# A decoder layer on one core: stages behind attention placed by lags and measured durations, queries turned two heads at a time

## The reference

```
x = x + layernorm(attention(layernorm(x))) * g2  # 16 query heads of 64, one shared key/value head, causal; q, k of unit length
x = x + cross_attention(layernorm(x), ctx)       # 16 heads of 16, no mask
x = x + experts(layernorm(x))                    # 4 experts, gate*sigmoid(gate)*value, hidden 1024; each token goes to the argmax expert
```

## Time and profile before

| | before |
|---|---|
| median of 3 runs | 1004.83 us (1004.71 to 1005.0) |
| profiled execution | 1004.88 us, of which the span of its instructions 1003.1 us |
| TensorE busy | 886.8 us, 88% |
| VectorE busy | 588.5 us, 59% |
| ScalarE busy | 580.2 us, 58% |
| GpSimd busy | 194.3 us, 19% |
| mean granted TensorE clock | 0.956 |

### The profile page before, as it was taken

One profiled execution on the slowest core, in us unless ns is written; L12 is line 12 of the kernel. 1 busy time (PEld: TensorE's weight loads), 2 busy tenths in 40 slices (PEclk: granted clock), 3 DMA queues, 4 the chain that ended last, 5 costly groups with the idle time before them and its releaser, 6 DMA issues.

```text
span 1003.1 us, 14623 instructions
## 1 busy us (share of the span) xinstructions
PE 886.8 (88%) x4510; PEld 676.9 (67%) x4510; DVE 588.5 (59%) x1369; ACT 580.2 (58%) x1144; POOL 194.3 (19%) x220
## 2 busy tenths in 40 slices
PE   4699999999999998889999999999771199999997
PEld 2566677677777775766777777776550178888885
DVE  4556778667677667667676676848586132323231
ACT  1586858778788776558686777778443022222221
POOL 3223221112111113113121111101103401111111
PEclk9799999999999999999999999999975599999999
DMA  8400000002000000000000000220123201010100
GB/s 274 79 2 1 1 1 1 1 1 85 1 1 2 1 1 0 1 1 1 1 1 1 1 1 1 88 81 1 64 93 122 84 1 33 19 32 21 32 16 10
DMA packets 19177, 29.04 MB, mean 29 GB/s; under 512 B 2079, under 2 KB 15648, under 8 KB 19104
## 3 DMA queue, kind: packets, MB, share of 16 engines
q1 hardware_dynamic: 17008, 22.73, 7.5%
q0 software_dynamic: 1680, 4.21, 1.2%
q10 hardware_dynamic: 416, 1.18, 0.3%
HBM read 21.41 MB, written 7.10 MB: 28 GB/s over the span
## 4 chain that ended last, share of the span: by engine, by line
PE 42%; DVE 4%; issue 3%; POOL 2%; ACT 1%; DMA 0%; DVEq 0%; ACTq 0%; POOLq 0%
PE W L1323 7%; PE S L1300 6%; PE O L1300 5%; PE O L1140 2%; PE S L1122 2%; PE S L1121 2%; PE O L1137 2%; PE O L1138 2%; PE W L1211 2%; PE W L1253 2%; POOL sorted_rows L602 2%; PE W L1233 1%; PE W L1179 1%; PE W L1311 1%; PE S L1311 1%
## 5 line engine op out<-in xcount | busy, mean ns | idle before, releaser
L860 DVE TENSOR_TENSOR pl<-pr,ph 128x512 fp32r<-128x512 f32 x288 | 199.5, 697 | 75.2 <-ACT pr L652 59.6
L651 ACT ACTIVATE ph<-S 128x512 fp32r<-128x512 f32 x288 | 174.1, 605 | 107.3 <-PE S L1122 104.0
L652 ACT ACTIVATE pr<-S 128x512 f32<-128x512 f32 x288 | 173.2, 601 | 0.0
L1137 PE MATMUL O<-ph,vhi 128*65 128x512 f32 x288 | 137.2, 476 | 0.0
L1140 PE MATMUL O<-pl,vhi 128*65 128x512 f32 x288 | 114.6, 398 | 10.0 <-DVE pl L860 9.7
L1122 PE MATMUL S<-qT,kT 128*128 128x512 f32 x288 | 114.0, 396 | 0.0
L1121 PE MATMUL S<-qT,kT 128*128 128x512 f32 x288 | 113.2, 393 | 0.0
L1138 PE MATMUL O<-ph,vlo 128*65 128x512 f32 x288 | 113.2, 393 | 0.0
L566 POOL TENSOR_TENSOR rn<-ssc,half 128x17 f32<-128x17 f32 x16 | 54.2, 3388 | 150.4 <-DVE ssc L891 145.1
L555 POOL TENSOR_TENSOR rs<-ri,half 128x1 f32<-128x1 f32 x48 | 36.7, 764 | 234.9 <-DVE ri L798 234.9
L768 ACT ACTIVATE gate<-S 128x512 f32<-128x512 f32 x38 | 20.6, 595 | 102.7 <-PE S L1300 102.7
(11 more groups left out here) (174 smaller groups left out, 1642.8 us busy)
## 6 DMA issues: line engine op xcount, KB each, us to landing
raw<-in_w_v SPq DMA_DIRECT2D x16, 512.0 KB, 4.0
wps<-in_w_proj SPq DMA_DIRECT2D x4, 1024.0 KB, 9.5
sorted_rows<-pad_row SPq DMA_DIRECT2D x19, 128.5 KB, 4.1
xs<-sorted_rows SPq DMA_DIRECT2D x19, 128.5 KB, 2.1
wqkv<-in_wqkv_t ACTq DMA_DIRECT2D x1, 1152.0 KB, 6.5
wout<-in_wout_t SPq DMA_DIRECT2D x1, 1024.0 KB, 10.0
xall<-in_x SPq DMA_DIRECT2D x1, 1024.0 KB, 11.0
xall<-in_x SPq DMA_DIRECT2D x1, 768.0 KB, 8.1
```

Of the source, the lines that this page charges most:

```text
L651: nc.scalar.activation(ph[:, k % RING, :], S[k % AHEAD][:], ACT.Exp, scale=SIM_SCALE).then_inc(ph_ready, 1)
L652: nc.scalar.activation(pr[:, k % RING, :], S[k % AHEAD][:], ACT.Exp, scale=SIM_SCALE)\
L860: nc.vector.tensor_tensor(pl[:, k % RING, :], pr[:, k % RING, :], ph[:, k % RING, :].bitcast(F32), ALU.subtract).then_inc(pl_ready, 1)
L1137: nc.tensor.matmul(o, vhi[:, vs, 0:DH + 1], ph[:, k % RING, :], start=j == 0, stop=False)
```

## The change

- **Order.** `STAGES` keeps only the stages ahead of and inside attention. The stages behind a tile's attention stand in `CHAIN`: each with the stage it follows and a lag in positions, counted from the tile's last attention step. `HAZARDS` lists for each the readers in an earlier tile that it must stay behind. `COST` holds a duration for each stage on VectorE, ScalarE and TensorE; a stage moves on to the next position while the two before, two after and its own hold more VectorE or ScalarE work than time. After the last slot come 90 positions without a step in place of three slots of eight. With lags summed, a tile's chain is 60 positions long.
- **Queries.** `q_high` and `qhl` go. `q_turn` turns the normed queries two heads at a time, in two stages of four transposes and one for the doubled key. ScalarE copies the high parts out of PSUM, even heads into rows 0 to 63 and odd heads into rows 64 to 127 of `qT`; `q_low`, now behind `q_turn` and on VectorE, subtracts them from the bank and writes each low part to the other half's rows. The bank is free after `q_low`. `lows_early` moves a `q_low` ahead of the stage that would need its bank. The value's low part is a subtraction on GpSimd.
- **Roots.** Each of the three kinds has its own ring of two.
- **Weights.** Eleven units in place of ten are split early, each behind a named stage of the last tile.
- Some small buffers move to other addresses.

```diff
-    ("heads_out", 3, -1, 1), ("probs_turn", 0, -3, 1), ("q_norm", 0, 1, 2), ("probs_turn", 1, -3, 2),
-    ("z2_turn", 0, -2, 3), ("q_norm", 1, 1, 3), ("out_turn", 0, -1, 5.5), ("probs_turn", 2, -3, 4), ("q_high", 0, 1, 4),
...
+    ("q_norm", 0, 1, 2), ("q_norm", 1, 1, 3), ("k_double", 0, 1, 4), ("v_parts", 0, 1, 5), ("q_turn", 0, 1, 7), ("q_low", 0, 1, 8),
+    ("norm_x", 0, 2, 7), ("heads_out", 0, 0, 9), ("z_turn", 0, 2, 11), ("q_turn", 1, 1, 11), ("q_low", 1, 1, 12),
+    ("q_turn", 2, 1, 14), ("q_low", 2, 1, 15), ("heads_out", 1, 0, 17), ("qkv", 0, 2, 19), ("qkv", 1, 2, 21),
+    ("qkv_squares", 0, 2, 22), ("qkv", 2, 2, 23), ("qkv_squares", 1, 2, 24), ("heads_out", 2, 0, 25),
+    ("qkv_sums", 0, 2, 26), ("qkv_sums", 1, 2, 28),
...
+CHAIN = [
+    ("heads_out", 3, None, 2), ("out_turn", 0, ("heads_out", 3), 4), ("out_turn", 1, ("out_turn", 0), 1),
+    ("out_proj", 0, ("out_turn", 1), 4), ("xa_norm", 0, ("out_proj", 0), 3), ("x1_stats", 0, ("xa_norm", 0), 3),
+    ("z2_norm", 0, ("x1_stats", 0), 3), ("z2_turn", 0, ("z2_norm", 0), 3), ("xq", 0, ("z2_turn", 0), 4),
+    ("scores", 0, ("xq", 0), 4), ("scores", 1, ("scores", 0), 1), ("probs_exp", 0, ("scores", 1), 1),
+    ("scores", 2, ("scores", 1), 2), ("scores", 3, ("scores", 2), 1), ("probs_exp", 1, ("scores", 3), 1),
+    ("probs_sum", 0, ("probs_exp", 0), 2), ("probs_sum", 1, ("probs_exp", 1), 2), ("probs_turn", 0, ("probs_exp", 1), 4),
+    ("probs_turn", 1, ("probs_turn", 0), 1), ("probs_turn", 2, ("probs_turn", 1), 1), ("probs_v", 0, ("probs_turn", 2), 4),
+    ("xo_turn", 0, ("probs_v", 0), 3), ("xattn_out", 0, ("xo_turn", 0), 4), ("x2_norm", 0, ("xattn_out", 0), 3),
+] + [("logits", e, ("logits", e - 1) if e else ("x2_norm", 0), 1) for e in range(EXP)]
+HAZARDS = {
...
+COST = {
...
+STEP = (0.7, 1.2, 1.16)
+IDLE = 1.5
+NEAR = 2
+TAIL = 90
...
+EARLY = {0: None, 1: ("out_turn", 0), 2: ("out_turn", 1), 3: ("xa_norm", 0), 4: ("z2_norm", 0), 5: ("z2_turn", 0), 6: ("xq", 0),
+         7: ("probs_sum", 1), 8: ("probs_turn", 0), 9: ("probs_turn", 2), 10: ("probs_v", 0)}
+EARLY_UNITS = len(EARLY)
...
+def lows_early(here):
+    owed = []
+    for stages in here:
+        n = 0
+        while n < len(stages):
+            name, part, t = stages[n]
+            if name in READER:
+                for entry in owed:
+                    entry[1] += 1
+                for key, _ in [entry for entry in owed if entry[1] >= WB]:
+                    for later in here:
+                        if key in later:
+                            later.remove(key)
+                    n = stages.index((name, part, t))
+                    stages.insert(n, key)
+                    n += 1
+                owed = [entry for entry in owed if entry[1] < WB]
+                if name == "q_turn":
+                    owed.append([("q_low", part, t), 0])
+            elif name == "q_low":
+                owed = [entry for entry in owed if entry[0] != (name, part, t)]
+            n += 1
...
+    load = [[sum(COST[entry[2]][e] for entry in entries) for e in range(3)] for entries in placed]
+    at_of = {}
+    def full(at, e, cost):
+        near = range(at - NEAR, min(at + NEAR + 1, last))
+        steps_near = sum(positions[n] is not None for n in near)
+        time = sum(load[n][2] + (IDLE if positions[n] is None else 0) for n in near) + (STEP[2] - STEP[e]) * steps_near
+        return load[at][e] > 0 and sum(load[n][e] for n in near) + cost > time
+    for t in range(TILES):
+        end = positions.index(start[GROUPS * (t + 1)] - 1)
+        for order, (name, part, behind, lag) in enumerate(CHAIN):
+            at = end + lag if behind is None else at_of[(*behind, t)] + lag
+            if t > 0:
+                at = max(at, at_of[name, part, t - 1])
+            for other, its_part, back in HAZARDS.get((name, part), []):
+                if t >= back:
+                    at = max(at, at_of[other, its_part, t - back])
+            while at < last and name not in ("heads_out", "out_turn") and any(COST[name][e] and full(at, e, COST[name][e]) for e in range(2)):
+                at += 1
+            at_of[name, part, t] = at
+            put(at, name, part, t, order)
+            for e in range(3):
+                load[at][e] += COST[name][e]
...
+                        nc.gpsimd.tensor_copy(vhi[:, vs, 0:DH], qn[:, HEADS + 1, :]).then_inc(v_ready, 1)
+                        pool.wait_ge(v_ready, 2 * t + 1)
+                        nc.gpsimd.tensor_tensor(vlo[:, vs, 0:DH], qn[:, HEADS + 1, :], vhi[:, vs, 0:DH].bitcast(F32),
+                                                ALU.subtract).then_inc(v_ready, 1)
...
-                        nc.scalar.copy(qhl[:, part * QH:(part + 1) * QH, 0, :], qn[:, part * QH:(part + 1) * QH, :])\
-                            .then_inc(qhi_ready, 1)
-                    elif name == "q_turn" and part < 4:
+                    elif name == "q_turn" and part < 2:
                         act.wait_ge(side_ready, job + 1)
                         if t >= 2:
                             act.wait_ge(s_ready, group_start[GROUPS * (t - 1)])
-                        nc.scalar.copy(qT[t % 2][:, 4 * part:4 * part + 4, :].rearrange("p h q -> p (h q)"),
-                                       W[job % WB][:]).then_inc(act_freed, 1)
-                    elif name == "q_turn" and part == 4:
+                        for rows, heads in halves_of(part):
+                            nc.scalar.copy(qT[t % 2][rows, heads, :], W[job % WB][rows, :].rearrange("p (h q) -> p h q", q=P))\
+                                .then_inc(qth_ready, 1)
+                    elif name == "q_turn" and part == 2:
                         act.wait_ge(side_ready, job + 1)
                         if t >= KV:
                             act.wait_ge(s_ready, group_start[GROUPS * TPB * ((t - KV) // TPB + 1)])
-                        nc.scalar.copy(kT[:, t % KV].rearrange("p a k -> p (a k)"), W[job % WB][:, 0:2 * P])\
-                            .then_inc(act_freed, 1)
+                        nc.scalar.copy(kT[:, t % KV, 0, :], W[job % WB][:, 0:P]).then_inc(qth_ready, 1)
...
+                    elif name == "k_double":
+                        dve.wait_ge(qn_ready, 2 * t + 2)
+                        if t >= 2:
+                            dve.wait_ge(side_ready, job_count("q_turn", 2, t - 2))
+                        nc.vector.tensor_copy(kdup[:, t % 2], qn[:, HEADS, :].unsqueeze(1).broadcast_to([P, 2, DH])).then_inc(kdup_ready, 1)
                     elif name == "q_low":
-                        heads = slice(part * QH, (part + 1) * QH)
-                        dve.wait_ge(qhi_ready, 2 * t + part + 1)
-                        nc.vector.tensor_tensor(qhl[:, heads, 1, :], qn[:, heads, :], qhl[:, heads, 0, :].bitcast(F32),
-                                                ALU.subtract).then_inc(qlo_ready, 1)
-                        if part == 1:
-                            dve.wait_ge(qlo_ready, 2 * t + 2)
-                            nc.vector.tensor_copy(kdup[:], qhl[:, HEADS].bitcast(F32).unsqueeze(2).broadcast_to([P, 2, 2, DH]))\
-                                .then_inc(kdup_ready, 1)
+                        bank = W[job_of["q_turn", part, t] % WB]
+                        if part < 2:
+                            for n, (rows, heads) in enumerate(halves_of(part)):
+                                other = slice(DH, P) if n == 0 else slice(0, DH)
+                                dve.wait_ge(qth_ready, 5 * t + 2 * part + n + 1)
+                                low = nc.vector.tensor_tensor(qT[t % 2][other, heads, :],
+                                                              bank[rows, :].rearrange("p (h q) -> p h q", q=P),
+                                                              qT[t % 2][rows, heads, :].bitcast(F32), ALU.subtract)
+                                low.then_inc(dve_freed if n else qtl_ready, 1)
+                        else:
+                            dve.wait_ge(qth_ready, 5 * t + 5)
+                            nc.vector.tensor_tensor(kT[:, t % KV, 1, :], bank[:, 0:P], kT[:, t % KV, 0, :].bitcast(F32),
+                                                    ALU.subtract).then_inc(dve_freed, 1)
...
-                        pe.wait_ge(qlo_ready, 2 * t + 2)
-                        pe.wait_ge(kdup_ready, t + 1)
+                        pe.wait_ge(qn_ready, 2 * t + (2 if part else 1))
+                        if part == 2:
+                            pe.wait_ge(kdup_ready, t + 1)
                         freed_wait(pe, job)
-                        for h in range(4 if part < 4 else 2):
-                            src = qhl[:, 4 * part + h].bitcast(F32) if part < 4 else kdup[:, h]
-                            mm = nc.tensor.transpose(W[job % WB][:, h * P:(h + 1) * P], src.rearrange("p a d -> p (a d)"),
-                                                     ident[:])
+                        for c in range(4 if part < 2 else 1):
```

(19 more changed lines are left out.)

200 lines of the change are left out of this document (94 added, 106 removed).

## The result

The changed kernel takes 997.63 us (median of four runs, 996.16 to 1001.04). The kernel before took 1004.77 beside it (1004.16 to 1005.0). The ratio is 0.9928, with a 95% interval from 0.9911 to 0.9945: faster by 7 us. The forecast was 20 us, so the direction was right and the size was off by 13. The profiled execution of after is the longest of its four (1001.04, with a span of 999.3; its mean granted clock was 0.939, that of the others 0.941, 0.944 and 0.944). The traces alone therefore differ by only 4 us, and sums from them stand some 3 us above the median.

The account below looks back on a forecast made before the run. TensorE was taken to bound the kernel, busy 88% of the span. 16.9 + 7 - 3 - 6.6 + 5.6 = 19.9 us saved, so 1004.9 - 19.9 = 985.0 us, range 969 to 999.

Parts of the forecast that it names:

- A bank is held longer: Turns' PSUM banks, held 1.9 to 2.7 us instead of 0.59: TensorE waits in six small tiles, 3 us lost.
- the granted clock 1.00 between 80 and 690: Sign of being right: TensorE keeps its full clock from 80 to 690 us, nearly all of attention.
- Rival C: Small tiles: bank waits cost 14.4 us instead of 3, no idle won beyond 5; 998.4 us, chance 0.14.
- B: Rival: small tiles fill up, no bank is waited for, tail set by dependencies alone; 965.6 us, chance 0.18.
- D: Rival: every turn, in large tiles too, makes TensorE wait for its bank; slower, 1010.8 us, chance 0.07.
- The transposes: TensorE turns 9 instead of 18 per tile and drops two of five turning stages: 16.9 us saved.
- The order: Chains spread over about 60 positions fill TensorE's idle time in small tiles: 7 us gained.
- Work that moves ahead: Work of tiles 13 and 14 moves from the tail into saturated attention: 6.6 us more TensorE time there.
- the tail: From last value matmul to last logit: tile 15's chain ends at 47 instead of 52.6 us, 5.6 less.
- VectorE's 24 us more: VectorE's extra subtractions, 1.5 us per tile, 24 in all: covered by its free time, counted at nothing.

Follow-up runs that it names:

- e1: Changed kernel with the low parts subtracted in SBUF, coming out zero, so ScalarE's copies free the bank: 981.88 us, 0.9756 of the kernel before.
- e3: Kernel before, its order of stages kept, with the new turn of the queries two heads at a time: 1005.04 us, 0.9994 of the kernel before.
- e9: Kernel before's order with the new turn and the bank freed by ScalarE's copies, low parts zero: 995.08 us, 0.9909 of the kernel before.
- e4: Changed kernel's new order with the old turn, queries split before they are turned: 1001.01 us, 0.9974 of the kernel before.
- e7: Changed kernel with the planner's shifts of stages off for tiles 12 to 15: 1005.96 us, 1.0000 of the kernel before.
- e10: e8 plus 24 needless matmuls in front of the last tile's stages in the tail: 990.46 us, 0.9856 of the kernel before.
- e8: Changed kernel with a turn's subtraction ahead of the very next job instead of the third: 990.41 us, 0.9846 of the kernel before.
- e2: Changed kernel with a turn's subtraction ahead of the second next job instead of the third: 991.32 us, 0.9852 of the kernel before.

## Why the prediction missed, by its own steps

**The step that failed** is "A bank is held longer: I take 3 us in all, because there TensorE has idle time already". The named waits are 11.2 us, and behind two of them TensorE ran slower, which the step priced at nothing and which "the granted clock 1.00 between 80 and 690" denied. Measured by e1, the held bank costs 15.7 us by the medians and 17 by the ratios. For the small tiles the 3 us were about right: 2.4. The reasoning failed for the large ones, at "three jobs take about 4 positions of 1.2 us or more: covered": 8.8 us of the waits are there, the longest of 3.03 in tile 7, which has 32 positions. That compared mean rates. The release stands in VectorE's queue behind other stages that themselves wait for TensorE (the timeline at 327 to 333). The bounds (0 to 38) held the cost, but they were worked out for the small tiles alone. Rival C, "the banks eat half", is what came, at 998.4 against 997.6, at a chance of 0.14. Its picture was right as to the bank, but it too placed the waits in the small tiles, and the clock's share wasn't in it: that its number fits is luck in part. Of the others, B needed no wait for a bank: e1 is that case, and its idle is 23.8, not the 13.6 that B wanted. D wanted every turn to wait, in large tiles too; 12 waits stand against its 48. Attention ended at 703.0, forecast 693.

Had I taken 15.7 in place of 3, the sum would have been 985.0 + 12.7 = 997.7, and 999 with 17; that the sum then fits so closely is luck, as the other terms show.

**The transposes** (16.9) held: 19.0 by after's trace, 19.5 by e1's, and in the old order 14.3 by e3's and 12.9 by e9's, all with the estimate for the clock in them. **The order** (7 of idle) held in kind: with the bank free, idle is 9.8 us under before's (23.8 against 33.6). In after the waits for the bank took as much again, and the idle time shows no change at all. With the old turn (e4) the order takes only 2.5 us of idle.

**Work that moves ahead** (6.6) was too large, and so was **the tail** (5.6). The step said that a chain is over in 60 positions. I read the lags and left out the shifts that the planner adds when an engine's surroundings are full. With them the chain of tile 13 takes 75 positions and that of tile 14 takes 64. Tile 13's product with the values still lies in the tail's first moments. The tail of after, as in the earlier trace rows, its last value matmul having ended at 703.0:

```profile
702.82 2.31 PE L1348 MATMUL W<-vb,pT 128*128 128x128 f32 x20
...
712.61 3.69 PE L1306 MATMUL W<-wout,onT 128*128 128x256 f32 x16 [1.76 <-DVE sc L1042]
...
726.87 1.92 PE L1320 MATMUL W<-z2T,wq 128*128 128x128 f32 x8
...
742.39 4.47 PE L1348 MATMUL W<-vb,pT 128*128 128x128 f32 x20 [1.10 <-ACT pT L823]
```

Only 20 records, some 2.2 us, went ahead. From the end of the last value matmul the projection starts at 9.6 (forecast 8.0, before 6.9), the query projection at 23.9 (19.7, before 22.8), the product at 39.4 (34.4, before 38.4). The scaling behind it no longer waits for other tiles' logits, as foreseen (43.9, forecast 37 to 39, before 44.4), but the product now runs at the low level, 4.47 for 2.42. The two errors nearly cancel: 6.6 - 5.6 was to cost 1.0 net, and 2.2 - 0.5 cost 1.7. In e4 tile 13's chain takes 64 positions, its product lies ahead of the last step, and the tail is 48.9, near the 47 of the forecast.

**VectorE's 24 us more** are not what made the change fall short: e1 has them too and is 17 us faster. In after the two subtractions of 689 ns take 1.41 from first start to last end, and the next instruction starts at 332.91: nothing overlaps, and some 0.03 us pass between two. The two of 753 in the earlier trace rows overlap by 0.085. Lost overlap is thus 0.115 us each. It isn't the wait that stands between the two subtractions: two `pl` of 128 rows with waits between them overlap too (in e1 1.29 us for two of 0.70, at 326.72). The Trainium skill, "VectorE: DVE Perf Modes", section "Two Vector instructions with no wait between them", has just this hold for an instruction on other partitions; my estimate from it was 0.08. The trace agrees in kind; e1 bears the same holds.

**What stays open.** e1 still spends 23.9 us of attention at the low level against 10.2 before, beside waits for `z`, `pl`, `sc` and `qn`. It isn't the new order's alone: e4 has 17.1 and e9 13.7. The two stretches near 120 and 160 us stand in every version with both the new order and the new turn, and in none with only one of them; no run took this apart. How much of the tail is owed to the clock is open as well (e4, e7, e10).

**The best whole version** is e8, the subtraction in front of the next job (e2 is within its spread): 0.9846 of before, against 0.9928 for the change as made. e1 shows that up to another 0.9% lies in a release that costs no engine anything. Going through SBUF doesn't reach it.

## What to carry to other kernels

When the reader of a shared buffer changes, price how long the buffer is then held, and follow the release through its engine's queue: what stands ahead of it, and whether that waits for the engine that wants the buffer. Do this in the dense stretches too, where mean rates say that there is time. Put such a release directly behind its producer, ahead of anything that waits. A short wait of TensorE in a saturated stretch can cost a second time, for the work behind it at the lower clock, but not each one does: compare several executions before putting a price on it. And read a planner's placement from its result, not from its table of lags.

## What the hardware showed that I had not expected

TensorE at 95% busy over attention (633 of 667 us) still fell to 1.2 GHz behind single waits of 1.6 to 3.0 us. Behind the wait of 2.49 for `qn`:

```profile
398.71 0.85 PE L1284 MATMUL W<-ident,qn 128*128 128x128 f32 x4 [2.49 <-DVE qn L982]
399.22 0.78 PE L1232 MATMUL O<-ph,vhi 128*65 128x512 f32 x1
399.79 0.63 PE L1233 MATMUL O<-ph,vlo 128*65 128x512 f32 x1
400.21 0.63 PE L1235 MATMUL O<-pl,vhi 128*65 128x512 f32 x1
```

The value matmuls, which take 0.47, 0.39 and 0.39 at full clock, take 0.78, 0.63 and 0.63. Other waits had no such effect: the same one of 3.03 in e7, and in after those of 1.29 at 210.57 and 1.13 at 561.63. Between after and e1 (11.2 us of waits for the bank, 13.6 us more of low clock) each us waited cost some 0.6 us again (6.8/11.2), an estimate from two traces.

Half the partitions didn't make an operation shorter. After's groups by line (as the earlier trace rows), 64 x 512 on VectorE and on ScalarE:

```profile
L996 DVE TENSOR_TENSOR qT<-W,qT 64x512 fp32r<-64x512 f32 x64 | 44.1, 689 | 10.7 <-ACT qT L776 8.9
...
L776 ACT CAST qT<-W 64x512 fp32r<-64x512 f32 x64 | 37.5, 585 | 17.5 <-PE W L1284 16.7
```

689 and 585 ns, beside 683 and 597 for 128 x 512 in the earlier trace rows. Splitting a 128-row operation in two by partition doubles its cost.
